# Logits of a dilated attention by column groups, experts centred singly, blank matmuls in a norm

## What is computed

```python
# dilated attention, for d in (1, 2, 3)
logits = einsum('bnc,bnkc->bnk', q, kw) * C ** -0.5      # kw: keys at n-d, n, n+d
attn = softmax(logits, axis=-1)
outs.append(einsum('bnk,bnkc->bnc', attn, vw))
out = mean(stack(outs)) @ Wproj + bproj
...
t = t + experts(ln(t))     # sum over 8 experts of weight * (gelu(x @ W1 + b1) @ W2 + b2)
t = t + causal(ln(t))      # this ln begins with the centring of the sum above
t = t + recurrence(ln(t))  # this is the last norm
```

## Time and profile before

| | |
|---|---|
| median of 3 runs | 409.14 us (409.04 to 409.5) |
| the profiled execution | 409.91 us, span 408.1 us |
| mean granted TensorE clock | 0.619 of full |
| busy: PE, DVE, ACT, POOL | 279.7, 255.5, 214.0, 17.3 us |
| chain that ended last: ACT, PE, DVE, issue | 39%, 33%, 15%, 10% |
| line 412 (ACT, recurrence) and line 727 (PE, recurrence) on that chain | 21% and 18% |

### The profile page before, as it was taken

How to read it: one execution, slowest core, us unless ns; L and a number is a source line. 1 busy time by engine, 2 the same in 40 slices (tenths; PEclk the granted TensorE clock), 3 DMA queues, 4 the chain that set the end, 5 groups by cost and what they waited for, 6 DMA issues and landing times.

```text
span 408.1 us, 12002 instructions
## 1 busy us (share of the span) xinstructions
PE 279.7 (69%) x3327; PEld 222.1 (54%) x3335; DVE 255.5 (63%) x2322; ACT 214.0 (52%) x1185; POOL 17.3 (4%) x29
## 2 busy tenths in 40 slices
PE   8898899897766666666666665666666665666663
PEld 3564467536655555555555555555555555555553
DVE  3885655625566666666666666666666666666665
ACT  2996452466555545554555555554555445554552
POOL 4006000023000000000000000000000000000000
PEclk9999996999555555555555555555555555555555
DMA  7500000000000000000000000000000000000000
GB/s 281 240 2 0 2 1 2 0 0 2 3 0 1 0 0 0 0 0 0 0 0 0 0 0 0 0 0 0 0 0 0 0 0 0 0 0 0 0 0 13
DMA packets 2972, 5.57 MB, mean 14 GB/s; under 512 B 1424, under 2 KB 1680, under 8 KB 2960
## 3 DMA queue, kind: packets, MB, share of 16 engines
q1 hardware_dynamic: 2672, 5.06, 3.3%
q10 hardware_dynamic: 288, 0.37, 0.3%
HBM read 5.29 MB, written 0.13 MB: 13 GB/s over the span
## 4 chain that ended last, share of the span: by engine, by line
ACT 39%; PE 33%; DVE 15%; issue 10%; DMA 1%; POOL 0%; SPq 0%; DVEq 0%; ACTq 0%; POOLq 0%
ACT bank L412 21%; PE bank L727 18%; ACT gi L400 11%; DVE ha L1025 6%; DVE terms_a L1025 5%; ACT bank L402 4%; PE bank L477 1%; PE bank L644 1%; PE bank L423 1%; PE bank L465 1%; PE bank L607 1%; DMA cst<-in_const 1%; PE bank L538 1%; PE bank L492 1%; PE bank L659 1%
## 5 line engine op out<-in xcount | busy, mean ns | idle before, releaser
L727 PE MATMUL bank<-ha,vparts 128*128 128x1 f16 x1536 | 96.0, 169 | 110.5 <-DVE ha L1025 110.5
L727 PEld LDWEIGHTS bank<-ha,vparts 128*128 128x128 f16 x1536 | 75.2, 107 | 133.3 <-DVE ha L1025 133.3
L400 ACT ACTIVATE gi<-bank 128x1 f32<-128x1 f32 x256 | 43.8, 171 | 145.5 <-PE bank L727 145.5
L412 ACT ACTIVATE bank<-bank,hc,gi 128x2 f32<-128x2 f32 x256 | 83.4, 326 | 0.0
L1022 DVE TENSOR_SCALAR go<-go 128x1 f32<-128x1 f32 x256 | 39.3, 154 | 66.1 <-ACT go L406 66.1
L727 PE MATMUL bank<-hb,vparts 128*128 128x1 f16 x768 | 76.6, 165 | 0.0
L727 PEld LDWEIGHTS bank<-hb,vparts 128*128 128x128 f16 x768 | 60.8, 104 | 0.0
L1025 DVE CUSTOM_DVE_ANT_0 terms_a<-bank,go 128x3 f32<-128x3 f32 x256 | 41.2, 161 | 29.1 <-ACT bank L412 0.2
L723 PE MATMUL bank<-x,w5s 128*128 (+1 forms) x198 | 56.6, 361 | 0.0
L520 PE MATMUL bank<-ones,w5s 128*128 128x8 f32 x198 | 55.9, 357 | 0.0
L1031 DVE SCALAR_TENSOR_TENSOR cell<-bank,gi,hc 128x1 f32<-128x1 f32 x256 | 54.9, 214 | 0.0
(11 more groups left out here) (213 smaller groups left out, 284.5 us busy)
## 6 DMA issues: line engine op xcount, KB each, us to landing
rel<-in_positions SPq DMA_DIRECT2D x4, 352.0 KB, 4.9
w3s<-in_w SPq DMA_DIRECT2D x1, 772.0 KB, 9.3
ltr<-in_later SPq DMA_DIRECT2D x1, 709.0 KB, 6.9
w2s<-in_w SPq DMA_DIRECT2D x1, 640.0 KB, 7.9
w5s<-in_w SPq DMA_DIRECT2D x1, 576.0 KB, 10.2
w0s<-in_w ACTq DMA_DIRECT2D x1, 336.0 KB, 4.0
w1s<-in_w SPq DMA_DIRECT2D x1, 256.0 KB, 7.0
w4s<-in_w SPq DMA_DIRECT2D x1, 192.0 KB, 10.2
```

The source lines that it names most:

```text
L400: act.activation(gi[:], bank[pre + 1][:, at:at + 1], ACT.Sigmoid, scale=1.0 / PRE)
L412: act.activation(tc_ends, gt.broadcast_to([P, 2]), ACT.Tanh, scale=gi[:], bias=hc[:]).then_inc(on("tanh_c"), 1)
L727: return mm(bank[3 * parity + k][:, at:at + 1], vparts[:, part, k], h, start=False, stop=False, skip_group_check=True)
```

## The change

- The constant `eighths` becomes 96 columns, three blocks of 32; in block d the columns 2d and 2d+1 hold the two images' channels.
- The logits of product (d, j) are now made with block d stationary and `qk` moving (256 columns), into partitions 32j to 32j+31 of `bank[1]`, adding up over d. VectorE copies 96 x 256 to `lrow`, TensorE transposes that by halves into `bank[2]`, and the softmax works on 36 numbers per partition in another order. The first value product stands behind the logits, the other two behind the transposes; three blanks follow instead of two.
- The third for the mean moves from `lw` into the widening, which becomes a `tensor_scalar` with an immediate.
- The fourth norm centres `t3part[3]` and then `ye[4]` to `ye[7]`.
- The last norm gets two blanks before the variances and two after.

```diff
-LATER = dict(group=P, eighths=B, dup0=P, diff=P, iota=E, onehot=E * P)
+LATER = dict(group=P, eighths=96, dup0=P, diff=P, iota=E, onehot=E * P)
...
+                if n == 5:
+                    keep_clock(var_bank[n][0], 2)
                 for h in range(HALVES):
                     pe.wait_ge(on("squares"), first + h + 1)
                     mm(var_bank[n][h][:, 0:B], sq[:, half[h]], c("means"), start=True, stop=True).then_inc(on("var_mm"), 1)
+                if n == 5:
+                    pe.wait_ge(on("dif"), first + 1)
+                    keep_clock(norm_bank[n][0], 2)
...
             for n in range(9):
                 pe.wait_ge(on("qk"), n + 1)
-                if n == 3:
-                    values_in(0)
-                if n == 6:
-                    values_in(1)
-                for h in range(HALVES):
-                    m = mm(bank[1][:, (n * HALVES + h) * B:(n * HALVES + h + 1) * B], qk[:, n // 3, n % 3, h * P:(h + 1) * P],
-                           c("eighths"), start=True, stop=True)
+                d, j = divmod(n, 3)
+                m = mm(bank[1][j * 32:(j + 1) * 32, 0:N], c("eighths")[:, d * 32:(d + 1) * 32], qk[:, d, j],
+                       start=(d == 0), stop=(d == 2), skip_group_check=True)
             m.then_inc(on("logit_mm"), 1)
+            values_in(0)
+            pe.wait_ge(on("lrow"), 1)
+            for h in range(HALVES):
+                m = pe.transpose(bank[2][:, h * 96:(h + 1) * 96], lrow[:, half[h]], ident[0:96, 0:96])
+            m.then_inc(on("logit_turned"), 1)
+            values_in(1)
             values_in(2)
-            keep_clock(bank[2], 2)
+            keep_clock(bank[1], 3)
...
-            for term, made, count in ((t3part[:, E - 3], "t3_part", E - 2), (ye[:, E - 2], "weighted", E - 1)):
-                pe.wait_ge(on(made), count)
+            pe.wait_ge(on("t3_part"), E // 2)
+            for h in range(HALVES):
+                mm(norm_bank[4][h][:, 0:P], c("centre"), t3part[:, E // 2 - 1, half[h]], start=True, stop=False,
+                   skip_group_check=True)
+            for e in range(E // 2, E - 1):
+                pe.wait_ge(on("weighted"), e + 1)
                 for h in range(HALVES):
-                    mm(norm_bank[4][h][:, 0:P], c("centre"), term[:, half[h]], start=(made == "t3_part"), stop=False,
+                    mm(norm_bank[4][h][:, 0:P], c("centre"), ye[:, e, half[h]], start=False, stop=False,
                        skip_group_check=True)
...
             dve.wait_ge(on("logit_mm"), 1)
+            dve.tensor_copy(lrow[:], bank[1][0:96, 0:N]).then_inc(on("lrow"), 1)
+            logits = bank[2][:, 0:HALVES * 96].rearrange("p (h j x) -> p h j x", h=HALVES, j=3)[:, :, :, 0:3 * B]
+            dve.wait_ge(on("logit_turned"), 1)
...
             for d in range(3):
-                stt(out=lw[:, d], in0=le2[:, d], scalar=1.0 / len(DIL),
-                    in1=lrec[:, d, None, :].broadcast_to([P, 3, HALVES * B]), op0=ALU.mult, op1=ALU.mult)\
-                    .then_inc(on("lw"), 1)
+                x = slice(d * B, (d + 1) * B)
+                tt(lw[:, d].rearrange("p j (h b) -> p h j b", h=HALVES), le2[:, :, :, x],
+                   lrec[:, :, None, x].broadcast_to([P, HALVES, 3, B]), ALU.mult).then_inc(on("lw"), 1)
             for d in range(3):
                 dve.wait_ge(on("lw"), d + 1)
-                dve.tensor_copy(wb[:, d].rearrange("p j h (b c) -> p (j h b) c", b=B),
-                                lw[:, d].rearrange("p j x -> p (j x)")[:, :, None].broadcast_to([P, 3 * HALVES * B, C]))\
-                   .then_inc(on("wb"), 1)
+                ts(wb[:, d].rearrange("p j h (b c) -> p (j h b) c", b=B),
+                   lw[:, d].rearrange("p j x -> p (j x)")[:, :, None].broadcast_to([P, 3 * HALVES * B, C]),
+                   1.0 / len(DIL), None, ALU.mult).then_inc(on("wb"), 1)
```

More of the change, by code:

```diff
@@ L145, in build @@
         qk = sb("qk", [P, 3, 3, N])
-        le, le2, lw = (sb(n, [P, 3, 3, HALVES * B]) for n in ("le", "le2", "lw"))
-        lmx, lsum, lrec = (sb(n, [P, 3, HALVES * B]) for n in ("lmx", "lsum", "lrec"))
+        lrow = sb("lrow", [96, N])
+        le, le2 = (sb(n, [P, HALVES, 3, 3 * B]) for n in ("le", "le2"))
+        lw = sb("lw", [P, 3, 3, HALVES * B])
+        lmx, lsum, lrec = (sb(n, [P, HALVES, 3 * B]) for n in ("lmx", "lsum", "lrec"))
         wb = sb("wb", [P, 3, 3, HALVES, P])
@@ L912, in _ @@
                     tt(qk[:, d, j], bank[3 + d][:, 0:N], kp[:, d, s:s + N], ALU.mult).then_inc(on("qk"), 1)
-            logits = bank[1][:, 0:9 * HALVES * B].rearrange("p (d j x) -> p d j x", d=3, j=3)
             dve.wait_ge(on("logit_mm"), 1)
-            link(dve.tensor_reduce(lmx[:], logits.rearrange("p d j x -> p d x j"), AX.X, ALU.max))
-            tt(le[:], logits, lmx[:][:, :, None, :].broadcast_to([P, 3, 3, HALVES * B]), ALU.subtract)\
+            dve.tensor_copy(lrow[:], bank[1][0:96, 0:N]).then_inc(on("lrow"), 1)
+            logits = bank[2][:, 0:HALVES * 96].rearrange("p (h j x) -> p h j x", h=HALVES, j=3)[:, :, :, 0:3 * B]
+            dve.wait_ge(on("logit_turned"), 1)
+            link(dve.tensor_reduce(lmx[:], logits.rearrange("p h j x -> p h x j"), AX.X, ALU.max))
+            tt(le[:], logits, lmx[:][:, :, None, :].broadcast_to([P, HALVES, 3, 3 * B]), ALU.subtract)\
                 .then_inc(on("shifted"), 1)
             dve.wait_ge(on("e2_ready"), 1)
-            link(dve.tensor_reduce(lsum[:], le2[:].rearrange("p d j x -> p d x j"), AX.X, ALU.add))
+            link(dve.tensor_reduce(lsum[:], le2[:].rearrange("p h j x -> p h x j"), AX.X, ALU.add))
             link(dve.reciprocal(lrec[:], lsum[:]))
             for d in range(3):
-                stt(out=lw[:, d], in0=le2[:, d], scalar=1.0 / len(DIL),
-                    in1=lrec[:, d, None, :].broadcast_to([P, 3, HALVES * B]), op0=ALU.mult, op1=ALU.mult)\
-                    .then_inc(on("lw"), 1)
+                x = slice(d * B, (d + 1) * B)
+                tt(lw[:, d].rearrange("p j (h b) -> p h j b", h=HALVES), le2[:, :, :, x],
+                   lrec[:, :, None, x].broadcast_to([P, HALVES, 3, B]), ALU.mult).then_inc(on("lw"), 1)
             for d in range(3):
                 dve.wait_ge(on("lw"), d + 1)
-                dve.tensor_copy(wb[:, d].rearrange("p j h (b c) -> p (j h b) c", b=B),
-                                lw[:, d].rearrange("p j x -> p (j x)")[:, :, None].broadcast_to([P, 3 * HALVES * B, C]))\
-                   .then_inc(on("wb"), 1)
+                ts(wb[:, d].rearrange("p j h (b c) -> p (j h b) c", b=B),
+                   lw[:, d].rearrange("p j x -> p (j x)")[:, :, None].broadcast_to([P, 3 * HALVES * B, C]),
+                   1.0 / len(DIL), None, ALU.mult).then_inc(on("wb"), 1)
             def weighted_value(n):
@@ L1053, in constants @@
     out["group"] = (groups[:, None] == groups[None, :]).astype(f) / (C // 8)
-    out["eighths"] = (batch[:, None] == np.arange(B)[None, :]).astype(f) * C ** -0.5
+    out["eighths"] = np.zeros((P, 3, 32), f)
+    for d in range(3):
+        out["eighths"][np.arange(P), d, d * B + batch] = C ** -0.5
     src, dst = np.arange(P)[:, None], np.arange(P)[None, :]
```

## The result

The changed kernel takes 405.58 us in the median of 20 executions (405.17 to 408.57), the kernel before 409.62 in 20 beside it (408.11 to 411.44). The ratio is 0.9922, with a 95% interval of 0.9900 to 0.9943: faster by 0.8%, or 3.2 us. That is the ratio of the two means, 406.55 and 409.76; the medians lie 4.0 us apart. The forecast was 404.3 us, 4.8 us less than 409.14, with a range of 403.1 to 406.3. The median lies in that wide range, but 0.3 us above 405.3, the upper end of the forecast's own range, and the gain by the means is two thirds of the forecast. One number doesn't describe it well: 12 of the 20 executions lie between 405.17 and 405.71, seven between 408.20 and 408.57, and one at 407.15. The kernel before spreads too, with five of its 20 near 411.3.

What follows compares the result with a forecast made beforehand. Bound: a recurrence of 256 dependent steps, three quarters of the span, after a chain of small waits between four engines. Terms -3.2 - 0.8 - 0.9 = -4.9 us; forecast 404.3 us against a median of 409.14, range 403.1 to 406.3.

Steps and rivals of the forecast that it cites:

- Part 1: Second layer's logits by column groups, third moved into the widening: reduction 3.1 us earlier, 3.2 us saved in all.
- two clock losses: TensorE's clock at half for about 7 us in the logits, and again from the last norm on.
- Part 2: Experts' centring waits only for GpSimd's fourth sum, TensorE centres experts 4 to 7 itself: 0.8 us saved, bounds 0.7 to 1.0.
- wait's 0.1: Experts' centring: 0.7 us saved instead of 0.8 if the first four passes carry this wait again.
- Part 3: Four blanks in the last norm hold the clock through the input products and first recurrence steps: 0.9 us saved.
- the input products: Six passes with the inputs before the recurrence: 1.38 us at half clock, 0.57 at full, 0.7 saved with the handover.
- the first steps: Recurrence: about three steps before the clock falls, each gaining 0 to 0.14 us; 0 to 0.4 together, taken as 0.2.
- the first rival: Clock falls in the last norm in spite of the blanks: 405.5 us, chance 0.22.
- The second pair's 0.25 us: Last norm: two blanks after the variances make the products that waited until 103.63 come 0.25 us later.
- The fourth rival: Clock falls in the experts, between 79.6 and 93.4 us: slower, 412 us with 8 us lost, chance 0.03.
- the first two rivals: Clock falls in last norm despite blanks, 405.5 us, chance 0.22; column groups overlap badly or widening slow, 406.0, chance 0.13.
- The third and the fifth rival: Logits don't keep the clock, 406.5 us, chance 0.05; clock full throughout the recurrence, about 392 us, chance 0.02.

Runs made afterwards that it cites:

- experiment 7: Changed kernel with three more blanks at the third norm and gate, all nine logit products in one column group (logits' values left out): 407.56 us, ratio 0.9957.
- experiment 2: Only the new centring of experts 4 to 7, on the kernel before: 409.10 us, ratio 0.9992.
- experiment 3: Only the last norm's four blanks, on the kernel before: 410.36 us, ratio 1.0013.
- experiment 10: Only three more blanks at the third norm and the gate, on the kernel before: 408.99 us, ratio 0.9982.
- experiment 1: Changed kernel with only the new logits and the third in the widening, experts' centring and last norm as before: 407.69 us, ratio 0.9942.
- Experiment 5: Changed kernel with three more blanks at the third norm and gate, without the last norm's four blanks: 405.58 us, ratio 0.9902.
- experiment 6: Changed kernel with three more blanks at the third norm and gate, without the last norm's two blanks after the variances: 405.15 us, ratio 0.9903.
- the three blanks: Added to the changed kernel: one before the third norm's squares, one after its variances, two instead of one at the end: 405.68 us, ratio 0.9895.
- experiment 9: Version of experiment 6 with two blanks of 504 columns behind each recurrence step's products, right values of the recurrence left out: 466.23 us.

## Why the prediction was right or wrong

- **Part 1, in the profile: right.** Forecast 3.1 us at the reduction and 3.2 with the rest. From the last query product's end to the reduction it is 3.06 us instead of 6.14, to the next norm's first product 11.63 (59.90 to 71.53) instead of 14.84 (59.72 to 74.56): 3.08 and 3.21. The groups overlap and VectorE sets the pace (experiment 7). The copy took 0.42 of a forecast 0.43, the two transposes 0.28 in the chain of 0.45. The widening did not slow down.
- **Part 1, as a gain of the kernel: too large, and this is the step that failed.** It is the reading "two clock losses: one of about 7 us in the logits", taken from one execution for the whole kernel, and with it the 3.1 us at the reduction that start from 65.86. Where in the stage the clock falls differs between executions. The same stretch of the old logits took 14.84 us in the profile of before, 14.32 in experiment 2 (59.85 to 74.17), 14.31 in experiment 3 (59.88 to 74.19) and 13.50 in experiment 10 (60.20 to 73.70). Against 11.63, the gain is 1.9 to 3.2 us, and the forecast used the upper end. The times agree: the shorter executions of experiment 1 have a mean of 406.60, the kernel before's lower 20 beside them 409.22, so part 1 is worth 2.6 us there, not 3.2.
- **Part 2: right in kind, 0.64 us instead of 0.8, just under its lower bound of 0.7.** Two terms were mis-sized, by 0.18 us together. The sixteen down passes keep TensorE for 1.88 us (88.35 to 90.23), not sixteen times 0.1125, a price taken from passes of 128 columns. The first group of four takes 0.55 us from start to start (90.23 to 90.78), not 0.45; the first group of the kernel before took as long, 0.54, behind a wait, which is the "wait's 0.1" of the forecast's bound. TensorE passes there from the down products' 64-column groups to full width, and the earlier trace rows had shown 0.14 for a change of grouping, which the sum for part 2 left out. The Trainium skill, "TensorEngine Tiling (Array Packing)", "Key Properties", says that a change of tiling mode drains the engine. No run here shows that this is what the 0.18 us are.
- **Part 3: the mechanism is there, the size isn't.** In the profile, the chain from the norm's first product to the first step's activation went from 5.09 (101.54 to 106.63) to 4.50 us, 0.6 instead of 0.9. Two terms fell short: the input products gave 0.55 us (1.38 to 0.83), not 0.7, and the first steps 0.01 each, not 0.2 together; that term came from a bound. And the gain exists only where the clock would be lost. The forecast took 1.38 for the case before, from one execution, and the first rival weighed only whether the blanks would fail, not whether the clock held without them. In experiment 1's profile, with the fall in the experts, it did hold, and the upper groups show the blanks as a cost of about 0.2 us there. Experiment 5 shows no gain at all. The second pair's 0.25 us was right (0.24, experiment 6).
- **The fourth rival, a fall in the experts, happened.** It had a chance of 0.03 and was meant as a new cost for all executions. In fact it strikes about four in ten of those with the new logits and without the three blanks, and about a third of the kernel before (31 of 97 above 410.5). It costs 2.7 to 2.9 us, not the 8 of the rival, because the clock came back after 6.8 us, as it had after the logits in the earlier trace rows. What spoke against it, "nothing in the change thins" that stage, was true. The thin stretch ahead of it was there before. No row of the third norm's and the gate's activity stood in the forecast, though the same reasoning that explained the logits pointed there.
- **Sum.** Profile against profile: 3.2 + 0.6 + 0.6 less 0.1 elsewhere is 4.3 us, where 4.9 was forecast. Typical execution against typical execution it is 3.8 (the 12 lowest of the changed kernel have a mean of 405.45, the 15 below 410.5 of the kernel before 409.23): 2.6 for part 1, 0.6 for part 2, 0.5 for part 3. Over all 20 executions of each it is 3.2, since the fall in the experts took more from the changed kernel in this series: 1.1 us of its mean, against 0.5.
- **Luck.** The range of 8 in 10 reached up to 406.3 for the sake of the first two rivals, and neither happened: the blanks held the clock, the groups overlapped, and the widening kept its rate. The first rival's number, 405.5, is almost the measured median, but for another reason. That the median lies in the range is luck to this extent. The third and the fifth rival didn't occur either.

## What to carry to other kernels

A profile shows one draw of a clock that falls at different moments in different executions. Before pricing a fall, list the stretches that look like those in which it fell in a profile (here matmuls of 2 and of 8 columns, each behind a load of 128), and treat each as a cost that some executions pay. Look at the single times, not only at their median, and compare a group of executions with the same group of the other kernel. A few blanks in such a stretch, in places where TensorE waits anyway, can be worth more than a shorter chain: here three of them removed a loss of 2.7 to 2.9 us that four executions in ten had. Blanks that stand in the chain cost something: the second pair in the last norm 0.24 us, two in each step of a loop at half clock 0.34 us in a step such as that shown in experiment 9.

## What the runs showed of the hardware

- A fully busy TensorE can lose the clock: it was busy for 3.30 of 3.30 us before the fall in the logits (experiment 2), with passes of two columns.
- In experiment 9 TensorE was busy all the time from 101.3 to 203.7, most of it with 504-column blanks (71.9 of 102 us), and the clock still stayed at half for 102 us. It was full from 203.7 to 224.1, then at half to the end. No experiment here explains it.
- A fall between 75 and 78 us lasted 6.8 us in each of the three profiles that have it, and then the clock was full again.
- Eighteen passes of 256 columns in three column groups took 2.13 us as VectorE delivered them, and 4.00 in one group.
- A recurrence step of one-column passes takes 1.15 us at full clock and 1.16 at half: its chain hardly depends on TensorE's clock (the changed kernel's profile).
